# Expert blocks of a fused graph-attention and mixture-of-experts kernel, handled two at a time

## The chip, the cores and the metric

The kernel runs on one core of a Trainium2 chip. The time is device microseconds from start to end of one execution; for the profiled execution the span of the core is given too. The core has five engines that each work through a queue of instructions of their own: TensorE (PE), VectorE (DVE), ScalarE (ACT), GpSimd (POOL) and SyncE (SP, which here only loads registers and issues transfers). They wait for one another by semaphores that are written out by hand in this kernel.

## The reference

Eight batches of 1024 tokens with 128 features go through a masked attention layer and then, after a layer norm, through a mixture of eight experts of which each token takes two. The part that the change touches:

```python
xf = x.reshape(-1, Dd)                       # 8192 tokens x 128, after a layernorm
probs = jax.nn.softmax(xf @ gate_w + gate_b, axis=-1)
top2_vals, top2_idx = jax.lax.top_k(probs, 2)
cw = zeros((N, 8)).at[arange(N)[:, None], top2_idx].add(top2_vals)
for e in range(8):
    h = gelu(xf @ W1[e] + b1[e])             # 128 -> 256
    out += cw[:, e, None] * (h @ W2[e] + b2[e])   # 256 -> 128
x = x + out
```

## The kernel before

The attention part ends at about 515 us of the span. Then the tokens are gated, and each token's row (128 features, its two norm factors, its two shares and its number, 133 values) is scattered to `rows_dram`, sorted by the pair of experts it takes. There are 28 pairs. GpSimd issues the scatters, the last at 646.67 us. Then the **expert stage** works on `BLOCKS` = 91 blocks of up to 128 rows, all rows of a block having the same pair of experts. This stage is all that the change touches.

For one block i:
- SyncE loads two registers (`block_at`: where the block's rows begin, and the number of its pair; L441), issues the transfer of the rows into a slot of `blk` (L447, DRAM to `ctx_sb`) and that of the two bias rows into `b2_ring` (L448, to `ctxT`). From block 8 on it first waits until the `combine` of block i-8 is done, which frees both slots. `AHEAD` = 8 is the depth of nearly all rings.
- VectorE normalises the rows (`blk_norm`, L1278).
- PE turns them (`turn_blk`, a transpose through L1410 into one of the two `side_ps` banks).
- ScalarE copies the turned block to f16, the high part (`blk_high`, L829); VectorE subtracts it and keeps the rest as the low part (`blk_low`, L1285).
- VectorE copies the first-layer weights of both experts from a table of all eight into a ring of four slots (`w1_copy`, L1300, 128x512 f16, written to `qk_hi`). The expert is picked by a register; the registers of four blocks are loaded at once (`load_experts`, L1293; the same on PE, L1664, and on ScalarE, L836).
- PE computes the first layers (`hidden`, once for each of the two experts; each of the two halves of the hidden layer takes three f16 products, high by high, high by low and low by high, L1414 to L1416, into `score_ps`, whose four banks are a ring). ScalarE applies the gelu (`gelu`, L845).
- PE computes the second layers (`second`: the bias product L1692, then L1694 to L1700, f32, two passes each, into one of two halves of `sum_ps`; it waits until the combine of block i-2 has been read out).
- VectorE makes the token numbers of the rows that are to be stored (L1307, `target`), and adds the two experts' outputs, weighed, to the rows (`combine`, L1311 and L1314, into `stage`). GpSimd scatters the result to the output (`store`, L576).

The order on each engine is that in which the code is written. PE, after the turns of blocks 0 to 2 and the first layers of 0 and 1, goes through: turn of i+3, first layers of i+2, second layers of i. VectorE: norm of i+4, registers at each fourth block, low part and two weight copies of i+3, combine of i. ScalarE: high part of i+1, then gelus of i.

## Time and profile before

| | us |
|---|---|
| median of 3 runs | 844.07 (842.79 to 844.43) |
| profiled execution | 843.84 |
| its span | 842.0 |
| PE busy in the span | 706.9 (84%) |
| VectorE busy | 734.3 (87%) |
| ScalarE busy | 579.9 (69%) |
| GpSimd busy | 556.8 (66%) |

The averages cover stages with different limits. The expert stage, from the first rows (issued at 650.0 us) to the last product (831.3 us), is to be read alone, by windows and by the timeline. In the timeline a row gives the start, the duration, the engine, the line, what is written and read, and in brackets how long the engine was idle before it and what ended that. A matmul's duration reaches past the start of the next one, since they are pipelined: what one costs is the distance between starts. A "q" behind an engine marks its sequencer, which loads registers and issues transfers.

### The profile page before, as it was taken

The numbers are of one execution on the slowest core, as the hardware profiler recorded it, in microseconds if no ns is written. First come the engines' busy times: TensorE is split into PE (matmuls) and PEld (weight loads), VectorE is DVE, ScalarE is ACT, GpSimd is POOL, SyncE is SP. The second block draws the span as 40 slices with busy tenths as digits, with TensorE's granted clock in tenths as the row PEclk, the third lists the DMA queues.
The fourth block names the chain that finished last, engine by engine and source line by source line (L and its number), as shares of the span: only waits on it lengthen the run. The fifth ranks groups of instructions, "written<-read, shape, count | busy, mean of one in ns | idle before, by whom it ended". The sixth has DMA issues, their size and how long they took to land.

```text
span 842.0 us, 20993 instructions
## 1 busy us (share of the span) xinstructions
PE 706.9 (84%) x6443; PEld 368.8 (44%) x6443; DVE 734.3 (87%) x2122; ACT 579.9 (69%) x1136; POOL 556.8 (66%) x570
## 2 busy tenths in 40 slices
PE   4598699999999999999999897647410799999994
PEld 2322133323233233332332234636410799999984
DVE  4989999999999999999999999885660599898884
ACT  4696587997987978978977775535300677777772
POOL 1212567887886987978878999677775255545553
PEclk9799899999999999999999998555655799999998
DMA  8915304205005023032050003001111122222220
GB/s 280 245 48 151 96 1 111 42 21 131 1 27 125 2 61 91 2 104 48 9 144 2 1 1 102 1 27 37 52 53 49 46 63 75 76 70 71 58 57 4
DMA packets 47599, 54.39 MB, mean 65 GB/s; under 512 B 7668, under 2 KB 31313, under 8 KB 47490
## 3 DMA queue, kind: packets, MB, share of 16 engines
q10 hardware_dynamic: 12672, 23.07, 10.5%
q1 hardware_dynamic: 29858, 21.41, 9.3%
q0 software_dynamic: 4960, 8.58, 3.1%
q8 instruction: 54, 0.88, 0.5%
q14 instruction: 55, 0.45, 0.2%
HBM read 34.03 MB, written 20.75 MB: 65 GB/s over the span
## 4 chain that ended last, share of the span: by engine, by line
PE 42%; DVE 31%; issue 9%; POOL 9%; DMA 3%; ACT 3%; SPq 2%; POOLq 0%; DVEq 0%; ACTq 0%
PE score_ps L1456 8%; DVE rspread L971 7%; PE sum_ps L1470 6%; PE side_ps L1486 6%; DVE prob_ring L950 6%; DVE w L950 6%; POOL rows_dram L569 4%; PE score_ps L1414 2%; DVE prob_ring L960 2%; PE sum_ps L1700 2%; PE score_ps L1415 2%; PE score_ps L1416 2%; PE sum_ps L1694 2%; PE sum_ps L1696 2%; PE sum_ps L1698 2%
## 5 line engine op out<-in xcount | busy, mean ns | idle before, releaser
L1456 PE MATMUL score_ps<-stack_mem 128*128 128x512 f16 x512 | 156.2, 388 | 20.2 <-DVE prob_ring L950 13.7
L723 ACT ACTIVATE prob_ring<-prob_ring 128x1024 f32<-128x1024 f32 x128 | 134.2, 1054 | 50.0 <-DVE prob_ring L950 39.2
L509 POOL TENSOR_TENSOR ctx_sb<-ctx_sb,rspread 128x512 f32<-128x512 f32 x108 | 139.2, 1289 | 41.7 <-DVE rspread L971 33.1
L723 ACT ACTIVATE w<-w 128x1024 f32<-128x1024 f32 x128 | 134.3, 1055 | 33.0 <-DVE w L950 32.2
L950 DVE SCALAR_TENSOR_TENSOR w<-score_ps,limit 128x1024 f32<-128x1024 f32 x128 | 152.7, 1211 | 4.1 <-PE score_ps L1456 3.9
L950 DVE SCALAR_TENSOR_TENSOR prob_ring<-score_ps,limit 128x1024 f32<-128x1024 f32 x128 | 153.2, 1202 | 0.9 <-PE score_ps L1456 0.7
L576 POOL DMA_INDIRECT out_x<-xn,limit x91 | 89.6, 985 | 97.0 <-DVE xn L1314 89.8
L514 POOL TENSOR_TENSOR ctx_acc<-ctx_acc,ctx_sb 128x512 f32<-128x512 f32 x93 | 119.1, 1281 | 7.3
L845 ACT ACTIVATE xn<-score_ps,vec 128x128 f32<-128x128 f32 x364 | 104.4, 369 | 20.3 <-PE score_ps L1416 20.2
L1456 PEld LDWEIGHTS score_ps<-stack_mem 128*128 128x128 f16 x512 | 29.3, 97 | 183.0 <-issue 82.5
L971 DVE STREAM_SHUFFLE rspread<-prob_ring 128x256 f32<-128x256 f32 x256 | 101.4, 448 | 0.0
L569 POOL DMA_INDIRECT rows_dram<-x,limit x64 | 63.9, 998 | 20.8 <-issue 19.3
L703 ACT ACTIVATE ctx_sb<-sum_ps 128x512 f32<-128x512 f32 x128 | 74.4, 582 | 1.8 <-PE sum_ps L1470 1.8
L829 ACT ACTIVATE xT_hi<-side_ps 128x128 f16<-128x128 f32 x91 | 25.3, 278 | 69.1 <-PE side_ps L1410 67.8
L1470 PE MATMUL sum_ps<-w,stack_mem 128*32 128x512 f32 x512 | 69.9, 619 | 0.0
L1414 PE MATMUL score_ps<-xT_hi,qk_hi 128*128 128x128 f16 x364 | 67.1, 222 | 2.1 <-DVE xT_lo L1285 1.2
L1470 PE MATMUL sum_ps<-prob_ring,stack_mem 128*32 128x512 f32 x512 | 68.2, 604 | 0.8 <-ACT ctx_sb L703 0.8
L1416 PE MATMUL score_ps<-xT_hi,qk_hi 128*128 128x128 f16 x364 | 67.2, 222 | 0.0
L1415 PE MATMUL score_ps<-xT_lo,qk_hi 128*128 128x128 f16 x364 | 67.2, 222 | 0.0
L1486 PE MATMUL side_ps<-w,gather 128*32 128x256 f32 x896 | 60.7, 389 | 0.0
L1486 PE MATMUL side_ps<-prob_ring,gather 128*32 128x256 f32 x896 | 60.0, 385 | 0.0
L1278 DVE TENSOR_SCALAR ctx_sb<-ctx_sb 128x128 f32<-128x128 f32 x91 | 31.1, 342 | 31.6 <-DMA ctx_sb<-rows_dram 31.3
(229 smaller groups left out, 1482.7 us busy)
## 6 DMA issues: line engine op xcount, KB each, us to landing
stack_mem<-qk_dram ACTq DMA_DIRECT2D x56, 256.0 KB, 4.5
ctx_sb<-rows_dram SPq DMA_DIRECT2D x91, 66.5 KB
qk_dram<-qk_hi ACTq DMA_DIRECT2D x16, 256.0 KB, 2.8
qk_dram<-qk_lo ACTq DMA_DIRECT2D x16, 256.0 KB, 3.9
x<-in_adj SPq DMA_DIRECT2D x4, 512.0 KB, 7.5
ctx_sb<-in_adj SPq DMA_DIRECT2D x4, 512.0 KB, 9.9
stack_mem<-qk_dram SPq DMA_DIRECT2D x16, 128.0 KB, 3.4
w<-in_L_ffn_W SPq DMA_DIRECT2D x4, 512.0 KB
```

Of the source, the lines that this page charges most:

```text
L509: pool.tensor_tensor(fresh, fresh, by, ALU.mult).then_inc(scaled_ready, 1)
L514: pool.tensor_tensor(ctxT[:, half, :] if k == T - 1 else ctx_acc[:], ctx_acc[:], fresh, ALU.add).then_inc(chunk_added, 1)
L569: pool.indirect_dma_start(rows_dram, bass.IndirectOffsetOnAxis(slot[:, t:t + 1], 0), x1_rows(t // T)[:, t % T, :], None, bounds_check=DUMM ...
L576: pool.indirect_dma_start(out_rows, bass.IndirectOffsetOnAxis(target[:, i % AHEAD:i % AHEAD + 1], 0), stage[:, i % AHEAD, :], None, bounds ...
L723: act.activation(prob_at(s, u), prob_at(s, u), ACT.Exp, scale=1.0 / SCORE).then_inc(exp_done, 1)
L845: ins = act.activation(hid[:, i % 4, e, k, :], score_ps[:, u % 4, k * P:k * P + P], ACT.Gelu, bias=vec[:, k, bass.ds(no, 1)], scale=1.0 / ...
L950: dve.scalar_tensor_tensor(out=prob_at(s, u), in0=score_ps[:, 2 * u:2 * u + 2, :], scalar=-LIMIT * SCORE, in1=limit[:, k:k + 1, half * HAL ...
L971: ins = dve.stream_shuffle(rspread[:, s % SPREADS, c * (HALF // 2):(c + 1) * (HALF // 2)], rinv[:], [2 * j + c] * DH)
L1415: pe.matmul(dst, a_hi, b_lo, start=False, stop=False)
L1456: ins = pe.matmul(score_ps[:, h, :], kstack[:, par, h, k * P:k * P + P], qstack[:, par, h, half * HALF:half * HALF + HALF], start=True, st ...
L1470: ins = pe.matmul(sum_ps[head, s % 2, :], v_sb[:, par, k, head], prob_at(s, h // 2)[:, h % 2, :], start=True, stop=True, tile_position=(0, ...
L1486: ins = pe.matmul(den_ps[DH * h:DH * h + DH, :], columns[:, j, 1 - c:DH + 1 - c], prob_at(s, h // 2)[:, h % 2, c * (HALF // 2):(c + 1) * ( ...
```

## The change

PE, VectorE and ScalarE handle the blocks in twos (`TWOS`, 46 of them, the last of one block). PE turns two blocks into one bank of `side_ps`, then does the first layers of the next two, then the second layers of two. The high and the low part and the token numbers of a two are one instruction each. The ring of rows has twelve slots (`ROWS`) where it had eight, and SyncE asks for the rows of block i+4 ahead of the biases of block i; the ring of weights has eight slots (`COPIES`), in `qk_hi` and `qk_lo`, where it had four. SyncE loads the registers of four blocks at once (eight registers), as the other engines did already. VectorE at the start copies the weights of four blocks and normalises six before the first low part, and in each pass of two does: low part of the two after next, registers, four weight copies, two norms (of the two after that), token numbers, two combines.

```diff
+    ROWS = 12
+    COPIES = 8
+    TWOS = [range(i, min(i + 2, BLOCKS)) for i in range(0, BLOCKS, 2)]
...
+            def load_places(c):
+                last = min(4 * c + 4, BLOCKS)
+                sp.load(places[c % 2][0:2 * (last - 4 * c)], row_table[0:1, 8 * c:2 * last])
+            def load_rows(i):
+                if i % 4 == 0:
+                    load_places(i // 4)
+                first = sp.snap(places[i // 4 % 2][2 * (i % 4)], min_val=0, max_val=DUMMY)
+                sp.dma_start(blk[:, i % ROWS, :], rows_dram[bass.ds(first, P), :]).then_inc(blk_loaded[i % ROWS], 16)
...
+            lead = ROWS - AHEAD
+            for i in range(lead):
+                load_rows(i)
             for i in range(BLOCKS):
-                sp.load(block_at, row_table[0:1, 2 * i:2 * i + 2])
...
                 if i >= AHEAD:
                     sp.wait_ge(target_ready, i - AHEAD + 1)
                     sp.wait_ge(rows_ready, i - AHEAD + 1)
-                sp.dma_start(blk[:, i % AHEAD, :], rows_dram[bass.ds(first, P), :]).then_inc(blk_loaded[i % AHEAD], 16)
...
+                if i + lead < BLOCKS:
+                    load_rows(i + lead)
+                load_b2(i)
...
-            def blk_high(i):
-                act.wait_ge(blk_turned, i + 1)
...
+            def blk_high(j):
+                r, n = TWOS[j].start % AHEAD, len(TWOS[j])
+                act.wait_ge(blk_turned, j + 1)
+                wait(act, z_done, 2 * (TWOS[j].stop - AHEAD))
+                act.activation(blk_hi[:, r:r + n, :], side_tiles(j % 2)[:, 0:n, :], ACT.Copy).then_inc(blk_hi_ready, 1)
...
+            for j in range(len(TWOS)):
+                if j % 2 == 0 and TWOS[j].start + 4 < BLOCKS:
+                    load_experts(j // 2 + 1)
+                for i in TWOS[j]:
+                    gelu(i, 0)
+                    gelu(i, 1)
+                if j + 2 < len(TWOS):
+                    blk_high(j + 2)
...
-                wait(dve, z_done, u - 3)
-                dve.tensor_copy(w1_ring[:, u % 4, :], w1_parts[:, bass.ds(4 * at, 4 * P)]).then_inc(w1_copied, 1)
+                wait(dve, z_done, u - COPIES + 1)
+                dve.tensor_copy(w1_slot(u), w1_parts[:, bass.ds(4 * at, 4 * P)]).then_inc(w1_copied, 1)
...
-            for i in range(2):
+            for i in range(4):
                 w1_copy(i, 0)
                 w1_copy(i, 1)
...
+            for j in range(3):
+                for i in TWOS[j]:
+                    blk_norm(i)
+            for j in range(2):
+                blk_low(j)
+            for j in range(len(TWOS)):
+                if j + 2 < len(TWOS):
+                    blk_low(j + 2)
+                    if j % 2 == 0:
+                        load_experts(j // 2 + 1)
+                    for i in TWOS[j + 2]:
+                        w1_copy(i, 0)
+                        w1_copy(i, 1)
+                if j + 3 < len(TWOS):
+                    for i in TWOS[j + 3]:
+                        blk_norm(i)
+                aim(j)
+                for i in TWOS[j]:
+                    combine(i)
...
+            def turn_two(j):
+                pe.wait_ge(blk_normed, TWOS[j].stop)
+                wait(pe, blk_lo_ready, j - 1)
+                for t, i in enumerate(TWOS[j]):
+                    ins = turn(side_tiles(j % 2)[:, t, :], blk_x2[:, i % AHEAD, :], ident[:])
+                ins.then_inc(blk_turned, 1)
...
             for i in range(BLOCKS):
-                if i + 3 < BLOCKS:
-                    turn_blk(i + 3)
-                if i + 2 < BLOCKS:
-                    hidden(i + 2, 0)
-                    hidden(i + 2, 1)
+                j = i // 2
+                if i % 2 == 0 and j + 2 < len(TWOS):
+                    turn_two(j + 2)
+                if i % 2 == 0 and j + 1 < len(TWOS):
+                    for n in TWOS[j + 1]:
+                        hidden(n, 0)
+                        hidden(n, 1)
```

What this makes of SyncE's queue is seen at the first blocks. `TENSOR_LOAD` is the register load, `ctx_sb<-rows_dram` the transfer of a block's rows, `ctxT<-b_dram` that of its biases; ISA rows are register arithmetic. Before:

```order
L441 TENSOR_LOAD limit
L442 ISA
L447 DMA ctx_sb<-rows_dram 128x133
L448 ISA
L448 DMA ctxT<-b_dram 2x256
L441 TENSOR_LOAD limit
L442 ISA
L447 DMA ctx_sb<-rows_dram 128x133
```

And now, in the same place:

```order
L458 DMA ctx_sb<-rows_dram 128x133
L451 TENSOR_LOAD limit
L457 ISA
L458 DMA ctx_sb<-rows_dram 128x133
L462 ISA
L463 DMA ctxT<-b_dram 2x256
L457 ISA
```

The first row here is the rows of block 3, the fourth row in a run with no biases between; the load is followed by the rows of block 4, and only then come the biases of block 0.

VectorE's queue in the middle of the stage, one block with a register load in it, before (norm, load, low part, two weight copies, token numbers, two sums):

```order
L1278 TENSOR_SCALAR ctx_sb<-ctx_sb 128x128
L1293 TENSOR_LOAD limit
L1285 TENSOR_TENSOR xT_lo<-side_ps,xT_hi 128x128
L1300 ISA
L1300 COPY qk_hi<-rspread 128x512
L1300 ISA
L1300 COPY qk_hi<-rspread 128x512
L1307 SCALAR_TENSOR_TENSOR limit<-ctx_sb,limit 128x1
L1311 SCALAR_TENSOR_TENSOR xn<-sum_ps,ctx_sb 128x128
L1314 SCALAR_TENSOR_TENSOR xn<-sum_ps,ctx_sb,xn 128x128
```

And now, a two (the same kinds of instructions, with the lines of the changed kernel):

```order
L1314 TENSOR_TENSOR xT_lo<-side_ps,xT_hi 128x256
L1322 TENSOR_LOAD limit
...
L1329 COPY qk_hi<-rspread 128x512
L1306 TENSOR_SCALAR ctx_sb<-ctx_sb 128x128 x2
L1337 SCALAR_TENSOR_TENSOR limit<-ctx_sb,limit 128x2
L1346 SCALAR_TENSOR_TENSOR xn<-sum_ps,ctx_sb 128x128
L1349 SCALAR_TENSOR_TENSOR xn<-sum_ps,ctx_sb,xn 128x128
L1346 SCALAR_TENSOR_TENSOR xn<-sum_ps,ctx_sb 128x128
L1349 SCALAR_TENSOR_TENSOR xn<-sum_ps,ctx_sb,xn 128x128
```

The load has moved behind the low part, the norms behind the four weight copies (one is shown).

## Rows read from the trace of the kernel before

**Rows 1.** Chain by line, then busy time of PE, PEld, DVE, ACT, POOL, clock, DMA; 740 to 760 us.

```profile
by line: PE score_ps L1414 12.4%; PE sum_ps L1696 11.2%; PE sum_ps L1694 11.2%; PE sum_ps L1698 11.2%; PE score_ps L1416 10.9%; PE score_ps L1415 10.9%; PE sum_ps L1700 10.7%; PE sum_ps L1692 5.5%; PE side_ps L1410 4.4%; issue 3.5%; DVEq L1
...
740.00:760.00 20.00, 19.47 (x239) 18.99 (x237) 18.11 (x77) 15.38 (x54) 9.95 (x11) 1.00 0.26 73
```

**Rows 2.** Timeline of PE, one block.

```profile
743.09 0.27 PE L1410 MATMUL side_ps<-ident,ctx_sb 128*128 128x128 f32 x1
...
743.20 0.22 PE L1414 MATMUL score_ps<-xT_hi,qk_hi 128*128 128x128 f16 x1
...
743.87 0.27 PE L1692 MATMUL sum_ps<-ctxT,unscale 128*128 128x256 f16 x1
...
744.87 0.27 PE L1410 MATMUL side_ps<-ident,ctx_sb 128*128 128x128 f32 x1
```

**Rows 3.** PE's register load (min/median/max ns), then bias products in the timeline.

```profile
L1664 PEldq TENSOR_LOAD <-limit x23: 587/591/831, 626.5 to 826.1; - x23
...
753.47 0.27 PE L1692 MATMUL sum_ps<-ctxT,unscale 128*128 128x256 f16 x1
755.39 0.27 PE L1692 MATMUL sum_ps<-ctxT,unscale 128*128 128x256 f16 x1
...
830.05 0.28 PE L1692 MATMUL sum_ps<-ctxT,unscale 128*128 128x256 f16 x1
```

**Rows 4.** SyncE's instructions by line (ns), then its timeline over one block.

```profile
L441 SPq TENSOR_LOAD <-limit x91: 687/705/891, 649.1 to 820.3; - x91
...
L447 SPq DMA_DIRECT2D ctx_sb<-rows_dram x91: 332/355/393, 650.0 to 821.3; - x91
...
742.67 0.35 SPq L447 DMA_DIRECT2D ctx_sb<-rows_dram  x1
743.21 0.27 SPq L448 DMA_DIRECT2D ctxT<-b_dram  x1
744.52 0.35 SPq L447 DMA_DIRECT2D ctx_sb<-rows_dram  x1
```

**Rows 5.** Waits from 660 us on (total, times, longest), then the latest such place.

```profile
DVE ctx_sb L1278 <- DMA ctx_sb<-rows_dram: 3.8, 4, 1.2
...
802.20 0.58 DVE L1278 TENSOR_SCALAR ctx_sb<-ctx_sb 128x128 f32<-128x128 f32 x1 [1.23 <-DMA ctx_sb<-rows_dram]
...
802.84 0.33 PE L1410 MATMUL side_ps<-ident,ctx_sb 128*128 128x128 f32 x1 [0.87 <-DVE ctx_sb L1278]
```

**Rows 6.** VectorE's register load (ns), the waits behind it, and one slow place.

```profile
L1293 DVEq TENSOR_LOAD <-limit x23: 594/599/848, 626.5 to 822.2; - x23
...
DVE xT_lo L1285 <- issue: 5.9, 21, 0.8
...
746.83 0.29 DVE L1285 TENSOR_TENSOR xT_lo<-side_ps,xT_hi 128x128 f16<-128x128 f32 x1 [0.77 <-issue]
...
747.45 0.22 PE L1414 MATMUL score_ps<-xT_hi,qk_hi 128*128 128x128 f16 x1 [0.53 <-DVE xT_lo L1285]
```

**Rows 7.** The start of the stage in the timeline, and the window in which the clock rises.

```profile
651.97 0.35 DVE L1278 TENSOR_SCALAR ctx_sb<-ctx_sb 128x128 f32<-128x128 f32 x1 [23.31 <-DMA ctx_sb<-rows_dram]
...
657.19 0.35 DVE L1278 TENSOR_SCALAR ctx_sb<-ctx_sb 128x128 f32<-128x128 f32 x1 [1.42 <-DMA ctx_sb<-rows_dram]
657.45 0.48 DVE L1285 TENSOR_TENSOR xT_lo<-side_ps,xT_hi 128x128 f16<-128x128 f32 x2
...
657.88 0.45 PE L1410 MATMUL side_ps<-ident,ctx_sb 128*128 128x128 f32 x1 [3.28 <-DVE xT_lo L1285]
...
662.40 0.42 PE L1692 MATMUL sum_ps<-ctxT,unscale 128*128 128x256 f16 x1
...
662.00:663.00 1.00, 1.00 (x9) 1.00 (x8) 0.24 (x2) 1.00 (x6) 0.00 (x0) 0.51 0.08 19
```

**Rows 8.** One of the two sums of a combine (ns), and GpSimd's last store.

```profile
L1311 DVE SCALAR_TENSOR_TENSOR xn<-sum_ps,ctx_sb x91: 336/351/352, 663.9 to 831.3; 128x128 f32<-128x128 f32 x91
...
833.33 0.97 POOL L576 DMA_INDIRECT out_x<-xn,limit  x1 [0.30 <-issue]
```

More of the change, by code:

```diff
@@ L1732, in _ @@
             at = weights_at(0, 0)
-            for i in range(3):
-                turn_blk(i)
-            for i in range(2):
+            for j in range(2):
+                turn_two(j)
+            for i in TWOS[0]:
                 hidden(i, 0)
```

89 lines of the change are left out of this document (33 added, 56 removed).

## The prediction, made before the changed kernel was run

> **What bounds the kernel now.** I read the windows of the end first, then the chain of waits, then the timeline of one block. The change lies wholly in the expert stage, which runs from about 650 us to 831 us of the span of 842.0. In it PE is busy for 19.5 of 20 us at a granted clock of 1.00, and VectorE for 18.1 of 20; the chain of waits goes from one PE instruction to the next, with VectorE pieces only where PE had stopped [rows 1]. So the stage costs what PE has to do, plus the places where PE stops.
>
> What PE has to do is seen between two turns of one block [rows 2]: the turn takes 0.11 us (743.09 to 743.20), the twelve products of the first layers 0.67 (to 743.87), the bias product and the eight passes of the second layers 1.00 (to 744.87): 1.78 a block. Every fourth block has 0.13 more (753.47 to 755.39 is 1.91 or 1.92), where PE loads the registers of four blocks; there are 23 such loads, 22 of them in this stretch [rows 3]. The second layers of block 0 start at 662.40 [rows 7], those of block 90 at 830.05 [rows 3]. Between these starts PE has 90 second layers, the first layers of blocks 3 to 90 and the turns of blocks 4 to 90: 90 x 1.00 + 88 x 0.67 + 87 x 0.11 + 22 x 0.13 = 90.0 + 59.0 + 9.6 + 2.9 = 161.5 us. It took 167.65. **PE stood for 6.1 us** in that stretch. Where?
>
> First cause, the rows. SyncE does for each block a load of two registers (705 ns), the issue of the rows (355 ns) and of the biases [rows 4]. The issue of the rows is followed 0.54 us later by that of the biases (742.67 to 743.21), and the next rows are issued at 744.52: 1.85 us a block, of which the register load and what surrounds it are about 0.77. PE needs a block each 1.78 + 0.13/4 = 1.815 us. SyncE is the slower of the two. It starts ahead (a first issue at 650.0) and loses a little on each block, until VectorE's norm, which has the rows, waits for the transfer: 3.8 us over four waits after the start, the longest at 802.20 after 1.23 idle; PE's next turn is then 0.87 late [rows 5]. Blocks spaced so are four, between 736 and 803, and by the spacing of the second layers they cost PE about 3.7 us in all.
>
> Second cause, VectorE's own register load (599 ns in the median, 848 at most) [rows 6]. It is in the queue ahead of the low part (L1285) that PE's next first layers but one need. Mostly VectorE idles 0.2 us there and PE notices nothing; at 746.83 it idled 0.77 and PE stood 0.53 until 747.45. Over all loads VectorE idles 5.9 us in 21 places. Four or five slow ones reach PE: the other 2.4 us of the 6.1.
>
> **The change part by part.** *PE in twos.* The instructions are the same: 91 turns, 364 threes, 91 bias products, 728 passes. Two turns in a row and two second layers in a row cost what they cost singly, so the sum by PE is not moved: 0. I see no row for two turns in a row at this clock; the bound above is 0.11 more each (a turn not overlapped), 46 x 0.11 = 5 us, the bound below 0. I take 0, since in rows 2 a turn already stands flush between unlike neighbours.
>
> *Slack of the low part.* Before, the low part of block i+2 is made in VectorE's pass i-1 and asked for by PE one pass later, 1.78 us. Now a two's low part is made a whole pass of two ahead: PE asks for it 3.56 us after its turn was issued. From the turn to the low part's end it takes about 0.9 to 1.4 us. A slow register load of 0.77 no longer reaches PE by that way. It is also queued behind the low part now, ahead of the copies; these are made two blocks ahead into eight slots. What is late next is the turn of the next two, whose norms stand behind low part, load and copies in the queue. From the last sum of the pass before to these norms VectorE has its whole work of a two less one combine. Work of a two: 18.11 us over 20/1.815 = 11.0 blocks is 1.64 a block, 3.29 a two [rows 1]; a combine is two of 351 ns, about 0.7 [rows 8]; 2.6 us are left, 3.4 with the slowest load, and PE comes to the turn 3.56 after. It fits. **Gain 2.4**, and perhaps 0.2 of it not.
>
> *VectorE's widths.* The low part of two blocks is one instruction of 256 columns for two of 128, the aim one for two. Either is at most twice its single price, so nothing is added; at best about 0.2 us a two are saved. VectorE isn't late, so 0. ScalarE: one wide copy for two, idle in the stage for a quarter of the time (15.4 busy of 20) [rows 1]: 0. The four more weight copies at the start stand where VectorE idles 23.3 us for the first rows [rows 7]: 0, and if that cover were gone, four of about 0.3.
>
> *SyncE.* A block costs now 2 x 0.54 for two issues and a quarter of a register load: 1.08 + 0.77/4 = 1.27 us, if a load of eight registers costs what a load of two does. The nearest rows are VectorE's and PE's loads of eight registers, 599 and 591 ns [rows 6, 3], no dearer than SyncE's of two, so I take that. From above, four times the load for four times the registers: 1.08 + (4 x 0.705 + 0.07)/4 = 1.80. 1.27 is well under 1.815, so SyncE goes back to waiting for free slots, and rows come more than four blocks early through the ring of twelve. **Gain 3.7.** The waits for free slots, in front of the rows of block i+4, ask for the combine of block i-8: the same lead of eight blocks that the biases had.
>
> PE's and VectorE's rows show eight registers in 0.59 us, SyncE's two in 0.71: no growth with the number. Against that stands a sentence of the Trainium skill, page "Runtime: NRT & Kernel Launch", section "Instruction fetch mechanics": a TENSOR_LOAD takes about 200 ns for each register, even in bulk. By it, as an estimate, SyncE's load of eight would be 1.6 us, and the sum below 1.8 us higher, as two such loads stand ahead of PE's start; the other engines' rows disagree with it by a factor of 2.7.
>
> *The start.* VectorE now does six norms ahead of the first low part (four before). Before: first rows issued at 650.0, normed at 651.97, 1.94 later; the fourth normed at 657.19 because SyncE comes once in 1.74 us; low part 657.45, PE's steady run from 657.88 [rows 7]. Now rows 0 to 3 are issued at 0.54 distance, 650.0 to 651.65, then a load (0.77), row 4 at 652.95, a bias and row 5 two steps on, 654.0. Its norm starts 1.94 later, 655.95, the low part 0.26 on, 656.2, and PE 0.43 after that (657.45 to 657.88) plus 0.12 to 0.29 for the double width: 656.8. **PE starts 1.1 earlier.** Its clock was granted at 0.51 in the window from 662 to 663, the low level of 1.2 GHz, and rose to the full one at the end of that window, while PE had run steadily from 657.88 [rows 7]. I let the rise move with the start, 1.1 earlier, to 661.9. Until the second layers of block 0 PE now has four first layers and two turns more, instead of one each: 4 x 1.34 + 0.44 = 5.8 at the low level (twice the times of rows 2), of which 5.1 are done between 656.8 and 661.9; the rest is 0.35 at full clock. The second layers of block 0 start at 662.2, about as before (662.40), but with one first layer and two turns more behind them.
>
> **Sum.** From 662.2: 90.0 + 87 x 0.67 + 85 x 0.11 + 22 x 0.13 = 90.0 + 58.3 + 9.4 + 2.9 = 160.6, so the second layers of block 90 start at 822.8, where they started at 830.05: 7.3 us less (6.1 of stalls, 1.2 at the start). I allow 0.2 for what a slow load still costs and for ScalarE's gelus just at the start: 7.1. What follows is unchanged: two sums, then GpSimd's last store at 833.33, 3.3 after, and its landing [rows 8]. The last three blocks stand in the same order in both. The profiled execution took 843.84 (span 842.0 and 1.84 around it); 843.84 - 7.1 = 836.7. The median of the runs is 844.07, 0.23 more: **837.0 us**.
>
> **Rivals.**
> (a) The register loads still reach PE: the low part is safe, but the norms behind the load aren't, since 2.6 + 0.77 + latencies touches 3.56. Then the 2.4 stay and the time is 839.4. For it: VectorE's 18.1 of 20. Against: only four loads are slow. 0.12.
> (b) SyncE's load costs by the register. Two loads stand ahead of the sixth rows, so the start loses twice what a load grows by: at twice today's 0.705, 1.4 us and 838.4; at four times, 4.2 us and 841.2, with SyncE's 1.80 a block just keeping up. For it: no row has SyncE loading eight. Against: the 591 and 599 of the others. 0.10 together. This is the rival that the skill's sentence above speaks for.
> (c) The change doesn't do what it says for one of its parts: PE's two turns or two second layers in a row open a gap of 0.05 to 0.1 at each of the 46 twos: 839 to 841.5. 0.08.
> (d) Slower: VectorE closes a loop. PE's turn waits for norms, these for the copies, these for the low part, that for the combine behind PE's last second layers. Its length is 2.6 to 3.4 now; it decides from 3.56, and from 3.56 + 0.16 per two (7.1/45) the kernel is no faster than before. That takes wide instructions or ring waits dearer by over 0.5 a two on VectorE. At 3.85: 45 x 0.29 = 13 more, 850. 0.04.
> (e) Better: the 0.13 at PE's loads shrinks too, since fewer waits stand around it: at half of it, 22 x 0.06 = 1.4, 835.5 and down to 834. 0.10.
>
> **How the numbers follow.** The forecast, 835.5 to 838.5, has 0.56, (a) to (e) the other 0.44. Its bounds: the start (0.5 either way), the remaining slow loads (up to 1), the spread of the runs (0.8). To hold 8 in 10 I reach up over (a), most of (b) and (c), and down into (e): 835.0 to 840.6. A measurement can tell about 0.2%, 1.7 us, from no change. Faster by more than that (under 842.4): 0.93; within: 0.03 (parts of b, c and d); slower: 0.04.
>
> **What the profile after would show.** SyncE's row issues 1.8 apart by waiting, not by working, and its load of eight under 0.9 us. No idle time of VectorE put down to the rows after the first six. Second layers in pairs 1.00 apart, pairs 3.56 apart, 3.69 at a register load, and no pair over 4. The second layers of block 0 near 662.2, the last near 822.9. It is wrong if PE waits at the turns of a two in each pair (loop d), if the load takes over 1.2 us, or if the first low part comes after 657.5.

## The result, and the profile after

| | before | after |
|---|---|---|
| median of the runs, us | 844.25 (842.79 to 846.58, 4 runs) | **834.19** (832.90 to 836.42, 4 runs) |
| profiled execution, us | 843.84 | 836.42 |
| its span, us | 842.0 | 834.6 |
| first rows of the stage issued | 650.03 | 652.85 |
| second layers of block 0 / of block 90 | 662.40 / 830.05 | 664.74 / 822.62 |
| start (first rows to second layers of block 0) | 12.37 | 11.89 |
| body (second layers of block 0 to those of 90) | 167.65 | 157.88 |
| stage (start and body) | 180.02 | 169.77 |

The changed kernel takes 0.9874 of the time of the kernel before (0.9857 to 0.9891). I forecast 837.0 with a range of 835.0 to 840.6: the direction was right, the gain was 10.1 us and not 7.1, and the time lies 0.8 under the range. The profiled execution's 836.42 stands close to the 836.7 that I worked out for it, but that is chance: its stage is 10.2 shorter, 3.1 more than forecast, and what comes ahead of the stage was 2.8 longer in it, which has nothing to do with twos. Two errors cancel in that one number. From here on, "start" and "stage" are measured from the first rows' issue and "body" from the second layers of block 0, so that what comes ahead stays out. In twos the start holds one first layer and two turns more and the body that much less, 0.67 + 2 x 0.11 = 0.9 us at the full clock; the stage is free of that shift.

The same window as in [rows 1]. PE has no idle time left (20.00 us busy, 19.47 before), and VectorE has less to do, 17.58 for 18.11, though it makes more blocks in the 20 us:

```profile
740.00:760.00 20.00, 20.00 (x244) 19.80 (x243) 17.58 (x67) 14.27 (x52) 10.98 (x12) 1.00 0.30 83
```

The bias products, which [rows 3] shows for before, open each block's second layers. They come in pairs, 1.00 apart in a pair and 3.56 from pair to pair, which is twice the 1.78 of a single block in [rows 2]. 3.56 is 2 x 1.00, 2 x 0.67 and 2 x 0.11, with nothing for the pairing:

```profile
739.57 0.27 PE L1732 MATMUL sum_ps<-ctxT,unscale 128*128 128x256 f16 x1
740.57 0.27 PE L1732 MATMUL sum_ps<-ctxT,unscale 128*128 128x256 f16 x1
743.13 0.27 PE L1732 MATMUL sum_ps<-ctxT,unscale 128*128 128x256 f16 x1
744.13 0.27 PE L1732 MATMUL sum_ps<-ctxT,unscale 128*128 128x256 f16 x1
746.69 0.27 PE L1732 MATMUL sum_ps<-ctxT,unscale 128*128 128x256 f16 x1
747.70 0.27 PE L1732 MATMUL sum_ps<-ctxT,unscale 128*128 128x256 f16 x1
```

Over the whole body only one pair comes later than that, by 0.09. The places with 0.13 more at every fourth block, which [rows 3] showed once (1.91 or 1.92 for 1.78), are gone as well, although PE and VectorE still make their 23 register loads, as long as before. The instructions by line of SyncE, VectorE and PE (min/median/max ns), to be set beside [rows 4, 6, 3]:

```profile
L451 SPq TENSOR_LOAD <-limit x23: 535/692/912, 651.9 to 802.6; - x23
...
L1322 DVEq TENSOR_LOAD <-limit x23: 595/599/845, 627.8 to 813.8; - x23
...
L1704 PEldq TENSOR_LOAD <-limit x23: 588/592/835, 627.9 to 818.1; - x23
```

SyncE's load of eight registers takes 692 ns, where the load of two took 705. What SyncE waits for between 660 and 830 us (total, times, longest) is now VectorE's combine, which frees a slot: SyncE is ahead.

```profile
SPq L472 <- DVE xn L1349: 48.4, 38, 3.0
```

The waits of the engines from 656 to 831 us answer to [rows 5, 6]. The rows are waited for three times, 1.7 us, all at the start. The wait of the low part (L1314) behind the register load has gone; VectorE idles ahead of the weight copies (L1329) and of the combine (L1346) instead:

```profile
DVE qk_hi L1329 <- PE score_ps L1454: 9.3, 22, 0.6
DVE xn L1346 <- PE sum_ps L1740: 8.1, 26, 1.0
...
DVE ctx_sb L1306 <- DMA ctx_sb<-rows_dram: 1.7, 3, 0.9
```

The first of these rows is not what it says. It has 22 times, once per register load; the load stands just ahead of the copies in the queue, and the first layers that it names had long been done when eight slots turn round. It is the load, 0.42 us a time. VectorE's timeline shows that this load costs nothing now:

```profile
741.77 0.35 DVE L1346 SCALAR_TENSOR_TENSOR xn<-sum_ps,ctx_sb 128x128 f32<-128x128 f32 x1 [0.27 <-PE sum_ps L1740]
742.16 0.35 DVE L1349 SCALAR_TENSOR_TENSOR xn<-sum_ps,ctx_sb,xn 128x128 f32<-128x128 f32 x1
742.43 0.41 DVE L1314 TENSOR_TENSOR xT_lo<-side_ps,xT_hi 128x256 f16<-128x256 f32 x1
743.25 0.96 DVE L1329 COPY qk_hi<-rspread 128x512 f16 x4 [0.41 <-PE score_ps L1454]
```

VectorE idles 0.41 at the load (743.25), catches up over the next two passes, and ahead of the next load it has time to wait 0.27 us for PE's second layers (748.90, as at 741.77). The price is paid out of slack.

The start, to be set beside [rows 7]: SyncE's five rows in one run of issues, the norms that wait for them, the first low part and PE's first product.

```profile
652.85 3.10 SPq L458 DMA_DIRECT2D ctx_sb<-rows_dram  x5
...
654.69 0.34 DVE L1306 TENSOR_SCALAR ctx_sb<-ctx_sb 128x128 f32<-128x128 f32 x1 [23.92 <-DMA ctx_sb<-rows_dram]
...
657.62 0.35 DVE L1306 TENSOR_SCALAR ctx_sb<-ctx_sb 128x128 f32<-128x128 f32 x1 [0.86 <-DMA ctx_sb<-rows_dram]
658.64 0.34 DVE L1306 TENSOR_SCALAR ctx_sb<-ctx_sb 128x128 f32<-128x128 f32 x1 [0.67 <-DMA ctx_sb<-rows_dram]
658.90 0.75 DVE L1314 TENSOR_TENSOR xT_lo<-side_ps,xT_hi 128x256 f16<-128x256 f32 x2
...
659.37 0.29 PE L1452 MATMUL score_ps<-xT_hi,qk_hi 128*128 128x128 f16 x1 [1.87 <-DVE xT_lo L1314]
...
664.00:665.00 1.00, 1.00 (x14) 1.00 (x12) 0.48 (x2) 1.00 (x6) 0.00 (x0) 0.72 0.28 70
```

The fifth and sixth norm (657.62, 658.64) stand ahead of the first low part, and PE waits for them through it. The granted clock, 0.50 in the windows that begin at 660 and at 662, averages 0.72 in this window and 1.00 in the next: if it stepped once from 0.50 to 1.00, that was at 664.56, 5.2 us after PE's first product.

### The profile page after: what moved, and what is told of

Same layout as the page of the kernel before. It is cut to its first block, busy times and chain, and to the rows that moved or that the text cites. A ratio compares the mean times of both kernels' runs of the same rounds, so it can differ in the third digit from the quotient of the medians.

```text
span 834.6 us, 20579 instructions
## 1 busy us (share of the span) xinstructions
PE 700.5 (84%) x6443; PEld 366.1 (44%) x6443; DVE 727.4 (87%) x2032; ACT 567.0 (68%) x1091; POOL 556.9 (67%) x570
## 4 chain that ended last, share of the span: by engine, by line
PE 43%; DVE 31%; POOL 12%; issue 10%; DMA 1%; ACT 1%; SPq 0%; POOLq 0%; DVEq 0%; ACTq 0%
PE score_ps L1494 8%; DVE rspread L999 7%; PE sum_ps L1508 7%; PE side_ps L1524 6%; POOL rows_dram L595 6%; DVE w L978 6%; DVE prob_ring L978 6%; PE score_ps L1452 3%; PE score_ps L1453 3%; PE score_ps L1454 3%; PE sum_ps L1734 2%; PE sum_ps L1740 2%; PE sum_ps L1736 2%; PE sum_ps L1738 2%; DVE prob_ring L988 2%
## 5 line engine op out<-in xcount | busy, mean ns | idle before, releaser
L1494 PE MATMUL score_ps<-stack_mem 128*128 128x512 f16 x512 | 158.3, 392 | 19.0 <-DVE prob_ring L978 13.4
L872 ACT ACTIVATE xn<-score_ps,vec 128x128 f32<-128x128 f32 x364 | 99.1, 383 | 11.4 <-PE score_ps L1454 10.3
L856 ACT ACTIVATE xT_hi<-side_ps 128x256 f16<-128x256 f32 (+1 forms) x46 | 17.6, 382 | 79.6 <-PE side_ps L1448 79.6
L1306 DVE TENSOR_SCALAR ctx_sb<-ctx_sb 128x128 f32<-128x128 f32 x91 | 27.7, 379 | 26.1 <-DMA ctx_sb<-rows_dram 26.0
L1448 PE MATMUL side_ps<-ident,ctx_sb 128*128 128x128 f32 x91 | 18.4, 284 | 30.2 <-DVE ctx_sb L1306 30.2
L519 POOL TENSOR_TENSOR x<-x,rows_bc 128x1024 f32<-128x1024 f32 x8 | 17.6, 2198 | 39.0 <-DMA gate_raw<-in_L_ffn_gate_w 21.4
L532 POOL TENSOR_TENSOR ctx_acc<-ctx_sb,rspread 128x512 f32<-128x512 f32 x16 | 20.6, 1285 | 31.0 <-DVE rspread L999 29.9
```

The costliest lines, as they stand in the source:

```text
L872: ins = act.activation(hid[:, i % 4, e, k, :], score_ps[:, u % 4, k * P:k * P + P], ACT.Gelu, bias=vec[:, k, bass.ds(no, 1)], scale=1.0 / ...
L1494: ins = pe.matmul(score_ps[:, h, :], kstack[:, par, h, k * P:k * P + P], qstack[:, par, h, half * HALF:half * HALF + HALF], start=True, st ...
```

## The experiments

Three things were open. Where did the 22 x 0.13 = 2.9 us go that I had put down to PE's own register load? Is SyncE's rate really the cause of the waits for rows? And is it the width of the work (twos) or the distance at which it is made ahead that takes VectorE's register load off PE's path? Theory A, as I first held it: what matters is that the load stands ahead of the low part in the queue. Its rival: any place in the queue costs the same, only the lead counts. Gains are given for the stage of the profiled execution; times are medians.

**The changed kernel again.** No edit.

> The changed kernel again, on the same chip as the three others. Stage 169.8 as in its first profile whatever the time before the stage does; that part (first rows issued at 650.03 in one profile, 652.85 in the other) is expected to vary by 2 us or so between executions of the same kernel, as nothing of it was changed but four weight copies. If the change itself had slowed it, the first rows would again be issued at 652.8.

835.10, ratio 0.9874 (0.9843 to 0.9904). Start 11.97, body 157.89, stage 169.86: the stage repeats to 0.1, the body to 0.01. The first rows were issued at 652.9 again.

**SyncE's registers four blocks at a time, in the kernel before.**

```diff
-                sp.load(block_at, row_table[0:1, 2 * i:2 * i + 2])
-                first = sp.snap(block_at[0], min_val=0, max_val=DUMMY)
-                pair_at = sp.snap(block_at[1], min_val=0, max_val=E * E - 1)
+                if i % 4 == 0:
+                    last = min(i + 4, BLOCKS)
+                    sp.load(places[i // 4 % 2][0:2 * (last - i)], row_table[0:1, 2 * i:2 * last])
+                first = sp.snap(places[i // 4 % 2][2 * (i % 4)], min_val=0, max_val=DUMMY)
+                pair_at = sp.snap(places[i // 4 % 2][2 * (i % 4) + 1], min_val=0, max_val=E * E - 1)
```

> The kernel before with one edit: SyncE loads the registers of four blocks at once, at each fourth block. No ring, order or width changes. Both theories: no waits of the norm for rows after the start, so 3.7 us less; the 1.91 spacings and the few slow VectorE loads stay; also the first four rows come somewhat earlier (the third and fourth by 0.7 each), so the start gains up to 1.5. Stage 175.0 to 176.3 against 180.0. If SyncE were not the cause of the row waits, they would stay at 3.8 us and the stage at 179 or more.

837.28, ratio 0.9903 (0.9874 to 0.9931). Start 9.73 for 12.37, body 163.69 for 167.65, stage 173.42: 6.6 us less, more than I had expected. The body's 4.0 are the waits for rows (I had 3.7); no wait for them is left in it. The other 2.6 are at the start, where the fourth row comes sooner. So this part alone carries two thirds of the change's gain. Its load of eight took 797 ns. The 0.13 at every fourth block stayed, and so did the place where it shows. In the waits of this kernel from 660 to 830 us:

```profile
DVE xT_lo L1287 <- issue: 5.9, 21, 0.7
...
PEld score_ps L1416 <- issue: 2.9, 16, 0.2
```

PE's weight load for the first product after a turn waits 16 times, 2.9 us. The kernel before has the same row for 670 to 820 us (L1414 there: 2.9, 16, 0.2), and its timeline shows one such place, inside the step of 1.91 of [rows 3]:

```profile
754.10 0.29 DVE L1285 TENSOR_TENSOR xT_lo<-side_ps,xT_hi 128x128 f16<-128x128 f32 x1 [0.22 <-issue]
...
754.69 0.10 PEld L1414 LDWEIGHTS score_ps<-xT_hi,qk_hi 128*128 128x128 f16 x1 [0.19 <-issue]
```

The missing 0.13 stands between the turn and the first products, behind the low part, and not at the second layers, ahead of which PE loads its registers.

**Whose register load is the 0.13?** Two kernels on top of the last one: one leaves out 22 of VectorE's 23 loads, the other 22 of PE's. They take the experts of blocks 0 to 3 for all blocks, so the work is the same and the outputs are not the reference's. Each was run once.

```diff
-                at = dve.snap(experts[i // 4 % 2][2 * (i % 4) + e], min_val=0, max_val=(E - 1) * P)
+                at = dve.snap(experts[0][2 * (i % 4) + e], min_val=0, max_val=(E - 1) * P)
...
-                    if (i + 3) % 4 == 0:
-                        load_experts((i + 3) // 4)
```

> The kernel with single blocks and SyncE's load of four (e2), from which VectorE's 22 register loads inside the stage are left out: it copies the first-layer weights of the experts of blocks 0 to 3 all the time, so the outputs are not those of the reference; the work is the same. Moving the load behind the low part had changed nothing, and there PE waited for the weight copies instead. Theory A2: VectorE has no slack in the order of single blocks (low part and weight copies are both made one pass before PE needs them), so its load costs PE 0.13 us wherever it stands, and more when it is slow. Without it no 1.91 spacings and no slow places: body (first to last second layers) 163.7 less 2.9 and less 1.9 to 2.4, so 158.4 to 159. Rival B (the 0.13 is PE's own register load): the 1.91 stay, body 161.5.

836.24. Start 9.85, body 159.18, stage 169.03. Up to the last blocks all spacings but three are 1.78 or 1.79. The same two steps as the 1.91 and 1.78 that the other kernel shows below (blocks 49 to 51):

```profile
L1295 DVEq TENSOR_LOAD <-limit x1: 837/837/837, 628.4 to 628.4; - x1
...
750.77 0.27 PE L1692 MATMUL sum_ps<-ctxT,unscale 128*128 128x256 f16 x1
752.55 0.27 PE L1692 MATMUL sum_ps<-ctxT,unscale 128*128 128x256 f16 x1
754.34 0.27 PE L1692 MATMUL sum_ps<-ctxT,unscale 128*128 128x256 f16 x1
```

VectorE's loads cost 4.5 us of body. With them, in SyncE's edit alone, there are 21 late steps at a distance of four blocks: sixteen by 0.13 (2.1 us) and five slow ones by 0.20 to 0.66 (2.2 us). ScalarE loads its registers in the same rhythm, and does so here too: its loads alone make no late step.

```diff
-                return pe.snap(experts[i // 4 % 2][2 * (i % 4) + e], min_val=0, max_val=(E - 1) * P)
+                return pe.snap(experts[0][2 * (i % 4) + e], min_val=0, max_val=(E - 1) * P)
...
-                    if (i + 1) % 4 == 0:
-                        load_experts((i + 1) // 4)
```

> The counterpart: single blocks and SyncE's load of four, with PE's 22 register loads inside the stage left out (it multiplies by the second-layer weights of the experts of blocks 0 to 3 all the time; outputs are not those of the reference). Theory A2: nothing changes, body 163.7 with 22 spacings of 1.91. Rival B, which is what the prediction said: the 0.13 goes, body 160.8.

837.26. Start 9.75, body 163.29, stage 173.04. The late steps at every fourth block are all still there, as is the row `2.9, 16, 0.2`:

```profile
L1666 PEldq TENSOR_LOAD <-limit x1: 777/777/777, 625.6 to 625.6; - x1
...
750.05 0.27 PE L1694 MATMUL sum_ps<-ctxT,unscale 128*128 128x256 f16 x1
751.96 0.27 PE L1694 MATMUL sum_ps<-ctxT,unscale 128*128 128x256 f16 x1
753.74 0.27 PE L1694 MATMUL sum_ps<-ctxT,unscale 128*128 128x256 f16 x1
```

The body is 0.4 shorter than with PE's loads, but at other places. PE's 22 loads cost 0.4 us in all, VectorE's 4.5. This pair refutes the step of the prediction.

**VectorE's load behind the low part, in the kernel before.**

```diff
                 if i + 3 < BLOCKS:
+                    blk_low(i + 3)
                     if (i + 3) % 4 == 0:
                         load_experts((i + 3) // 4)
-                    blk_low(i + 3)
                     w1_copy(i + 3, 0)
```

> The kernel before with one edit: VectorE's register load stands behind the low part of block i+3 instead of ahead of it. All times are of the stage, from the issue of the first rows to the start of the bias product of block 90: 180.0 us before (650.03 to 830.05), 169.8 after (652.85 to 822.62). Theory A: the 0.13 us at every fourth block, which the prediction put down to PE's own register load, comes from VectorE's load ahead of the low part; with it moved, the spacing of second layers has no 1.91 any more, and the slow places at ordinary rows are gone too. SyncE still needs 1.85 a block, so rows become the bound: the waits of the norm for rows grow from 3.8 us to 8 or more, and the stage is 178.3 (the last rows issued 171.3 in, landing 1.9, turn 0.5, then 4.5 of PE's work). Rival B (the 0.13 is PE's own load): the 1.91 spacings stay, 22 of them, row waits grow by 1 us or so, the stage is 178.5 to 179.

844.66 over ten runs, ratio 0.9999 (0.9980 to 1.0019). Body 167.64 for 167.65. The steps of 1.91 stay. This alone could still be SyncE's rate taking back what was won, so both edits were put together.

**Both of these edits in the kernel before.**

```diff
+                if i % 4 == 0:
+                    last = min(i + 4, BLOCKS)
+                    sp.load(places[i // 4 % 2][0:2 * (last - i)], row_table[0:1, 2 * i:2 * last])
...
+                    blk_low(i + 3)
                     if (i + 3) % 4 == 0:
                         load_experts((i + 3) // 4)
-                    blk_low(i + 3)
```

> The two edits together, on the kernel before: single blocks, rings of eight and four, single low parts. Theory A: PE runs without a stop, all spacings 1.78, stage 158.6 from the first second layers to the last plus 11.0 to 12.4 ahead of it: 169.6 to 171.0, so the twos and the longer rings bring 1 us or nothing beyond the two moved loads. Rival B (PE's load costs 0.13): 172.5 to 174. Rival C (the slack of single blocks is too small, the low part still comes late now and then): more than 172, with waits of PE on the low part at 1.78 + x.

838.71, ratio 0.9931 (0.9907 to 0.9955). Start 9.73, body 163.70, stage 173.44, as with SyncE's edit alone (173.42), 2.4 over the upper end of what theory A expected. The waits tell why:

```profile
DVE qk_hi L1302 <- issue: 6.4, 21, 0.6
...
744.65 0.77 DVE L1302 COPY qk_hi<-rspread 128x512 f16 x2 [0.62 <-issue]
...
745.01 0.10 PEld L1416 LDWEIGHTS score_ps<-xT_hi,qk_hi 128*128 128x128 f16 x1 [0.60 <-issue]
```

The idle time of VectorE has moved from the low part to the weight copies behind it, and PE now waits for the copies (its weight load at 745.01 stood 0.60), which in single blocks with four slots it needs just as soon. Theory A falls.

**The load ahead of the low part, in the changed kernel.** The opposite test.

```diff
                 if j + 2 < len(TWOS):
-                    blk_low(j + 2)
                     if j % 2 == 0:
                         load_experts(j // 2 + 1)
+                    blk_low(j + 2)
```

> The changed kernel with VectorE's register load put ahead of the low part again. Theory A2: lead matters and not the place in the queue, so body 157.9 as in the changed kernel. Against it: 161 or more, with the 0.13 back.

836.16 in its only run. Start 11.88, body 157.79, stage 169.67, 0.1 less than the changed kernel, which is what that kernel's own two profiles differ by. With the longer lead the place in the queue makes no difference either.

**Single blocks, but one block more ahead.** On top of SyncE's four: turns, high parts, low parts and copies are made one block earlier, into eight weight slots. No twos.

```diff
-                wait(dve, z_done, u - 3)
+                wait(dve, z_done, u - COPIES + 1)
...
-                if i + 3 < BLOCKS:
-                    if (i + 3) % 4 == 0:
-                        load_experts((i + 3) // 4)
-                    blk_low(i + 3)
-                    w1_copy(i + 3, 0)
-                    w1_copy(i + 3, 1)
+                if i + 5 < BLOCKS:
+                    blk_norm(i + 5)
+                if i + 4 < BLOCKS:
+                    blk_low(i + 4)
+                    if (i + 4) % 4 == 0:
+                        load_experts((i + 4) // 4)
+                    w1_copy(i + 4, 0)
+                    w1_copy(i + 4, 1)
...
-                if i + 3 < BLOCKS:
-                    turn_blk(i + 3)
+                if i + 4 < BLOCKS:
+                    turn_blk(i + 4)
```

> Single blocks and SyncE's load of four, with one more block of lead: turns, high and low parts and weight copies four blocks ahead instead of three, weights in a ring of eight; rows ring of eight, no twos, no wide instructions. Theory A2 (it is lead, not width, that the twos bring): spacings all 1.78, body 157.9 to 158.3; with the start of single blocks (9.8 us from the first rows to the first second layers, maybe 1 more for the fourth low part) a stage of 167.7 to 169, that is 1 to 2 us less than the changed kernel's 169.8. If wide instructions are needed to give VectorE room, the 1.91 stay: body 161 or more.

837.14, ratio 0.9887 (0.9870 to 0.9905). Body 159.92, of which one first step of 3.05; hardly any other is over 1.80, and none is over 1.82. VectorE still idles at its load, PE no longer waits for anything that VectorE makes. In the waits from 670 to 820 us no row of PE is left, and this one of VectorE:

```profile
DVE qk_hi L1307 <- issue: 5.9, 23, 0.5
```

So the lead takes the load off PE's path, not the width. Its start is worse, 12.67 for 9.73, and takes back 2.9 of the body's 3.8; the stage is 172.59 for 173.42, and the medians don't tell the two apart. The first product comes as early as there (5.9 us after the first rows for 5.8). The time goes behind it: ScalarE makes the fourth high part ahead of its first gelu, and PE turns that block only behind four first layers, which fill the four banks that the gelus have to empty. PE waits 2.73 us for the first gelu:

```profile
659.99 0.28 ACT L836 ACTIVATE xT_hi<-side_ps 128x128 f16<-128x128 f32 x1 [2.38 <-PE side_ps L1417]
...
662.79 0.22 PE L1421 MATMUL score_ps<-xT_hi,qk_lo 128*128 128x128 f16 x1 [2.73 <-ACT xn L852]
```

**VectorE's load twice, in the changed kernel.** This was to measure the slack left.

```diff
                 dve.load(experts[c % 2][0:2 * (last - 4 * c)], pe_table[0:1, 8 * c:2 * last])
+                dve.load(experts[c % 2][0:2 * (last - 4 * c)], pe_table[0:1, 8 * c:2 * last])
```

> The changed kernel in which VectorE loads its expert registers twice each time (0.6 us more at every fourth block). Theory A2: in twos VectorE has lead of a whole pass, so a delay that its idle time (0.41 and 0.27 at every second pass) takes up later costs PE nothing: body 157.9 to 159. If the twos only just fitted, PE would lose up to 0.5 at each, body up to 168.

833.21 in its only run, start 11.89, body 157.88, stage 169.78. It tells nothing of the slack. The trace has 23 loads of VectorE, as without the edit:

```profile
L1323 DVEq TENSOR_LOAD <-limit x23: 594/597/844, 624.6 to 810.5; - x23
```

The first of the two writes registers that nobody reads before the second does, and it is not in the executed program. What ran was the changed kernel a third time. How much more VectorE could bear was not measured.

**SyncE's registers for each block, in the changed kernel.** The rest of the change without SyncE's part.

```diff
-            def load_places(c):
-                last = min(4 * c + 4, BLOCKS)
-                sp.load(places[c % 2][0:2 * (last - 4 * c)], row_table[0:1, 8 * c:2 * last])
+            def load_place(i):
+                at = 2 * (i % 4)
+                sp.load(places[i // 4 % 2][at:at + 2], row_table[0:1, 2 * i:2 * i + 2])
...
-                if i % 4 == 0:
-                    load_places(i // 4)
+                load_place(i)
```

> The changed kernel with SyncE loading two registers for each block again. SyncE then needs about 1.85 a block against PE's 1.78, and although rows are asked for four blocks further ahead the ring gives it no rate: body 157.9 plus what the queue lacks. From the first rows, the rows of block 90 are issued after 90 x 1.86 = 167.4 less the bias transfers of the last four, and end about as in the kernel before: stage 172 to 176 against 169.8, with waits of the norm for rows in the last third. The start is later by four to six loads less two, about 3 us. Rival (the longer ring hides it): stage under 171.

835.44 in its only run. Start 13.50, body 158.18, stage 171.68: only 1.9 more, with 1.6 of it at the start, and no waits for rows behind the start. I had expected them to come back. SyncE's loads by line, and two of its steps:

```profile
L451 SPq TENSOR_LOAD <-limit x91: 470/646/805, 649.1 to 807.2; - x91
...
700.43 0.34 SPq L457 DMA_DIRECT2D ctx_sb<-rows_dram  x1
700.96 0.29 SPq L462 DMA_DIRECT2D ctxT<-b_dram  x1
702.17 0.34 SPq L457 DMA_DIRECT2D ctx_sb<-rows_dram  x1
```

A block costs SyncE 1.74 here, where it was 1.85 in [rows 4], with a load 59 ns shorter in the median. PE takes 1.78. So the waits for rows in the kernel before hung on 0.07 us a block, and the same loads in a slightly different loop are just fast enough. The rest lies around the load: from its end to the issue of the rows it is 0.29 in the kernel before (743.52 + 0.71 to 744.52), where a wait for the free slot stands there, and 0.18 here (701.35 + 0.64 to 702.17), where that wait stands ahead of the load and costs 0.08. The longer ring asks for rows earlier as well, but the rate suffices without it: from the issue of a block's rows to their norm it was 5.8 us at block 6 of the kernel before and 2.5 at block 42; here it is 5.9 at block 7 and 4.4 at block 89, a loss of 1.5 over the whole stage.

**The first low parts ahead of the fifth and sixth norm, in the changed kernel.**

```diff
-            for j in range(3):
+            for j in range(2):
                 for i in TWOS[j]:
                     blk_norm(i)
             for j in range(2):
                 blk_low(j)
+            for i in TWOS[2]:
+                blk_norm(i)
```

> The changed kernel with one edit at its start: the first two low parts ahead of the norms of blocks 4 and 5, as PE's first layers wait for the low part and those norms wait for rows. In the changed kernel the first low part comes at 658.90, 6.05 us after the first rows are issued (652.85), the norm of block 3 at about 656.4 to 656.8. Theory: PE starts 1.7 us earlier, its clock rises earlier by as much, start 10.2 instead of 11.9, stage 168.1 instead of 169.8, body unchanged at 157.9. Rival: PE then waits at the third turn for the norm of block 5 and the gain is under 0.5.

**832.00**, ratio 0.9823 (0.9806 to 0.9841): the lowest median of this study. Start 9.35 for 11.89, body 158.17 for 157.88, stage 167.52 for 169.77. The low part comes 4.0 after the first rows instead of 6.1, and PE's first product with it:

```profile
656.86 0.42 DVE L1314 TENSOR_TENSOR xT_lo<-side_ps,xT_hi 128x256 f16<-128x256 f32 x1
...
657.34 0.29 PE L1454 MATMUL score_ps<-xT_hi,qk_hi 128*128 128x128 f16 x1
```

Of the 2.5 that the start gains, 2.1 lie ahead of that product. The first rows were issued at 652.9 in this profile as well. One step of the body grew by 0.28, the second pair's, since its rows' norms now come last.

**That kernel, with GpSimd's first addition held back.** Of the 2.8 us ahead of the stage, 1.4 are there when PE starts its first attention scores (35.47 us before, 36.88 after), and they go with one place near 24.5 us. (At the last scores it is 2.1, 507.39 and 509.45; what adds the rest is not shown.) GpSimd adds a 128x1024 tile while VectorE writes masks. In the profile of before the addition took 3.71 us and the masks 0.69 each; after, one mask took 3.41 and the addition 2.25. The instructions by tile, the masks and the additions of after (L519's shortest and longest, and L1041's):

```profile
L1041 DVE TENSOR_SCALAR w<-ctx_sb x4: 676/716/3409, 24.0 to 28.6; 128x1024 bf16<-128x1024 int32 x4
...
L519 POOL TENSOR_TENSOR x<-x,rows_bc x8: 2185/2188/2250, 24.5 to 425.2; 128x1024 f32<-128x1024 f32 x8
```

and of before:

```profile
L1013 DVE TENSOR_SCALAR w<-ctx_sb x4: 685/686/687, 23.8 to 25.6; 128x1024 bf16<-128x1024 int32 x4
...
L493 POOL TENSOR_TENSOR x<-x,rows_bc x8: 2181/2194/3711, 24.6 to 423.1; 128x1024 f32<-128x1024 f32 x8
```

Neither line is touched by the change. In every profile of this study up to here one of the two is long: VectorE's in five (first rows issued at 652.6 to 653.3), GpSimd's in eight (649.6 to 652.7, so the place doesn't set that time alone). Which one is long goes with a few tenths of a microsecond. In the five, the addition starts before the second of these four masks, and that mask is the long one; in the eight it starts after the second mask has started, and GpSimd waits for all four.

```diff
             pool.wait_ge(rows_loaded, 16 * 5)
+            pool.wait_ge(mask_made, T)
             add_beta(0)
```

> The version with the early low parts (e7) plus one wait far from the stage: GpSimd's first addition of 128x1024 (it starts at 24.5 us) waits until VectorE has made the masks. In the four profiles in which the first rows were issued at 652.8 to 653.3 with a first score product late, one mask instruction of VectorE takes 3.4 us where it takes 0.69, beside this addition at 2.2 us; in the others the mask instructions take 0.69 and GpSimd's addition 3.4 to 3.8. Theory: only one of the two can have its way, and when VectorE is the one held, everything after is 2.7 us late. Apart, all mask instructions take 0.69 and the addition 2.2, the first rows are issued at about 650.2 and the time is 2 to 2.7 under e7's 832.0: 829.3 to 830. Rival (the lateness has another cause, such as the length of the program): first rows at 652.8 again.

832.53, ratio 0.9851 (0.9824 to 0.9877). Kept apart, both are short, as expected.

```profile
L1042 DVE TENSOR_SCALAR w<-ctx_sb x4: 685/685/686, 24.2 to 26.0; 128x1024 bf16<-128x1024 int32 x4
...
26.87 2.18 POOL L519 TENSOR_TENSOR x<-x,rows_bc 128x1024 f32<-128x1024 f32 x1 [23.73 <-DVE w L1042]
```

The first rows were issued at 651.5, 1.4 earlier than without it. But the median is not lower than 832.00, where I had expected 829.3 to 830, and neither is the ratio. Either the gain is given back later, or the kernel without it has VectorE's long instruction in its profile and not in most of its other executions. The second can happen: the kernel with the doubled load, which ran as the changed kernel, had GpSimd's long and its first rows at 649.6, where the changed kernel itself had them at 652.85 and 652.9. The runs don't decide, and this stays open.

## Why the prediction was right in direction and short by three

By its own steps.

**What PE has to do**: right, 1.78 a block, and the twos add nothing. With the 0.13 left out, the sum for the body is 90.0 + 58.3 + 9.4 = 157.7; it took 157.88. Rival (c), a gap at each two, fell.

**The step that failed is the term 22 x 0.13 = 2.9 us.** I saw the step of 1.91, saw that PE loads registers at that distance [rows 3], and wrote the 0.13 to PE's load, as work that PE has to do in both kernels. VectorE loads in the same rhythm [rows 6]. The first kernel of the pair above, without VectorE's loads, has no such steps; the second, without PE's, has them all. What the steps cost is 21 x 0.13 = 2.7, as there are 21 of them and not 22. The profile of before already held what was needed: within the step, the 0.13 lies between the turn and the first product, and the weight loads there wait in 16 places, as many as there are plain late steps in that stretch (that 16 waits of 0.18 also make 2.9 is chance). "Mostly VectorE idles 0.2 us there and PE notices nothing" was wrong: PE noticed 0.13 of each. With the term taken out of the sum the same prediction gives 834.1, where the median is 834.19. That it fits to a tenth is luck: its stage would be 170.1, and 169.77 was measured.

Rival (e) had the sign, with the cause named wrongly and half the size as its main case: 835.5, down to 834, and a chance of 0.10. Nearly the whole term went, and my range ended at 835.0, half way into it.

**The slow loads, 2.4**: right in cause, and they went with the lead, as I had it. But with the 2.9 they would make 5.3, and without VectorE's loads the body fell 4.5 below SyncE's edit alone. The slow places' 2.2 there has their own 0.13 in it, which my sum counted once more. That the load was moved behind the low part gave nothing by itself.

**SyncE, 3.7**: right in cause and size for the body, 4.0 when done alone. The load of eight costs 0.69 (0.80 in the kernel before with this edit alone), so rival (b) fell. That holds as well against the sentence of the Trainium skill on about 200 ns for each register (page "Runtime: NRT & Kernel Launch", section "Instruction fetch mechanics"): eight registers would be 1.6 us by it, and two 0.4, where 0.69 and 0.71 were measured. The page speaks of registers loaded from HBM, and this kernel's table lies in SBUF; no run here loads registers from HBM. What I did not see is how narrow it was: 1.85 against a need that, without the 0.13, is 1.78.

**The start, 12.2**: measured 11.89. Two of its steps held: low part 6.2 after the first rows (6.05), PE's first product 6.8 (6.52). The rise of the clock, put at 5.1 after that, came after 5.2, but this is chance, for it does not move with PE's start: the granted clock rose 2.8 us after the first product in SyncE's edit alone, 4.2 with the early low parts and 1.8 in the kernel after that one. And the sum hid a loss. SyncE's edit alone shortens the start to 9.73, and the twos take 11.89. With four norms ahead of the first low part where the change has six, the same twos start in 9.35, and their stage is 2.3 shorter. I had costed the two added norms only as an offset to the faster rows and never asked what the start would be without them.

**VectorE's loop, rival (d)**: not reached. A two takes 17.58/20 x 3.56 = 3.13 us of VectorE's time, a little under the 3.29 that I took from before, and once per four blocks VectorE waits for PE. Rival (a) fell with it.

**Around the stage**: I left it unmoved. In the median it was (10.1 in all, 10.2 in the stage); in the single profiled execution it was not.

## What to carry to other kernels

A small extra that recurs with a period shared by several engines belongs to none of them until it is placed: find the two instructions between which it lies, and read what the second one needed, before writing it down as the work of the engine that shows it. An instruction in a saturated engine's partner (a register load of 0.6 us here) is hidden by making things further ahead, not by shifting it within the queue. And look at a change's parts one at a time: here one part, four blocks' registers in one load, brought 6.6 us by itself, where the whole change brought 10.2, and another, the two norms more ahead of the first low part, cost 2.3.

## What the runs showed of the hardware that I had not expected

GpSimd's 128x1024 fp32 addition and VectorE's 128x1024 int32 to bf16 mask instruction do not run side by side: 0.69 us became 3.41, or 2.19 became 3.71, and which of them pays differs between profiles. The Trainium skill has the rule (page "SBUF — State Buffer", section "Who interferes with whom"): the two engines share a port pair, an instruction of VectorE that uses both its pairs (a `tensor_scalar`, as the masks are, can) contends for it with GpSimd, the first to issue holds it for its whole instruction, and the other blocks. The trace agrees for VectorE if GpSimd's next instructions are counted in. The mask of 3.41 began at 24.64 and the addition ended at 26.75, which alone would make 2.8; but GpSimd's sixteen memsets follow the addition at once, and the mask ended at 28.05, its own 0.69 after 27.4. That the memsets held it is read from these times and was not tested:

```profile
26.70 0.33 POOL L504 MEMSET rank<- 128x1 f32 x8
...
27.30 0.20 POOL L508 MEMSET earlier<- 128x128 bf16 x1
```

For GpSimd the trace shows more than the rule gives: in the profile of before the addition began at 24.62, within the second mask, waited until the fourth ended at 26.29 and not only for the one that it met, and ended 2.0 later, at 28.33. In all thirteen profiles it ends 2.0 to 2.1 us after the end of a mask, the first in the five and the fourth in the eight.

A register load on SyncE costs about the same for two registers (646 and 705 ns in two loops) as for eight (692 and 797), and on PE and VectorE eight cost 0.59 and 0.60. PE's load, at a saturated PE, cost 0.4 us for 22 of them.
